# First attention: the division by the sums moved from VectorE to a ScalarE copy of the used columns and a GpSimd power and product

## Chip, cores and metric

One core of one Trainium2 chip. The metric is the device time of one launch in microseconds; the time is the median of the runs. One more execution, recorded by the profiler, gives the profile and the trace; its own time stands beside them below.

## The reference

Four layers follow each other, each added to its normalised input. Only the first attention is touched, and the time of the others counts with it:

```python
def _L0_attn_ref(x, ln_gamma, ln_beta, w_qkv, b_qkv, w_out, b_out):    # x: 4 x 1024 x 128, 16 heads of 8
    residual = x
    h = (x - mean(x)) * rsqrt(var(x) + 1e-05) * ln_gamma + ln_beta
    q, k, v = split_heads(h @ w_qkv + b_qkv)
    scores = einsum('bhqd,bhkd->bhqk', q, k) / sqrt(8)
    attn = softmax(scores)
    out = einsum('bhqk,bhkd->bhqd', attn, v)
    return residual + merge_heads(out) @ w_out + b_out

x = L0_attn_x
x = x + _L0_attn_ref(_layernorm(x), ...)
x = x + _L0_ffn_ref(_layernorm(x), ...)     # a shared expert and 8 routed ones, the best 2 of each row
x = x + _L1_attn_ref(_layernorm(x), ...)    # differential attention, 8 heads
x = x + _L1_ffn_ref(_layernorm(x), ...)     # linear layers on values quantised to 4 bits
```

The softmax is exp(score - maximum) divided by the sum of the exponentials. The kernel multiplies the undivided exponentials with the values and divides the result: each head has 8 columns of results and one column of sums.

## The kernel before

**Engines and order.** All four compute engines and the DMA queue of SyncE run through one list of steps (`plan_all`). Each engine takes from it, in this order, the steps in which it has a part, and every step's part stands in a function of the step's name, one per engine. Engines meet through semaphores: `SIGNALS` says which step raises which and by how much, `READ` says which signal tells that a step's PSUM bank has been read, so that the bank's next user may write it. All waits are counts worked out from the list. An engine never runs past a wait.

**The planner.** In the first attention time is counted in slots. A slot has one `maxima` step and, six steps of eight slots later, one `scores` step. `hook(s, slot, step)` puts a step at a given slot. Steps named in `BEHIND_SUMS`, `divide` among them, are held back and put directly behind the next `burst`, at most two at a time. `FOLLOWS` names steps that the planner adds a number of slots after another one has been put (`later`, `tick`). PSUM banks are given out in a ring: `maxima` and the other steps in `RINGED` share four banks (0 to 3), `scores` and the steps in `RINGED_ACT` share three (5 to 7), and bank 4 collects the results.

**Units.** A unit `u` (0 to 15) is one block of 1024 rows (`b = u // 4`) and four of its sixteen heads (`gr = u % 4`). It has these steps:

- `maxima(u, t, j, half)`, 64 in all: TensorE multiplies 128 queries of head j with 512 keys (L1705), VectorE takes the maximum of each row from PSUM (L1274, tile a_mx). `row1(u, c)` joins them (L1281), `row2(u, c)` turns them on TensorE (L1711) and ScalarE copies them out twice (L828, L829); `row2_low` subtracts the rounded copy on GpSimd (L2071) and writes both into the queries' extra rows by two DMAs (L2188). The scores of the next unit wait for these.
- `scores(u, hs, j)`, 64: TensorE (L1717), then ScalarE's exponential from PSUM into tile a_PT (L836). In the last half unit two of them are joined into a `pair` of 1024 columns (L1727, L844).
- `burst(u, c, k)`: TensorE multiplies the exponentials of mostly three tiles with values and a column of ones (L1743). After the last burst of each half c, ScalarE copies the collected results to tile a_OT (L851).
- `divide(u, r)`, two for each unit and so 32: TensorE turns 512 columns of a_OT by four transposes into a ring bank (L1751): 4 row tiles of 4 heads of 32 columns, of which 8 are results, the ninth is the sum, and the others aren't used. VectorE takes the reciprocals of the 16 sums (L1288, tile a_rc) and multiplies the 128 results with them into tile a_Oa (L1292).
- For the last unit of a block, `turn_o(b, r)`: TensorE turns a_Oa (L1758), ScalarE copies (L857), and `out_project(b, r)` multiplies (L1766) and adds to the residual on VectorE (L1300).

**What lies beside it.** The next block's norms are worked out during its predecessor's second unit: statistics on VectorE (`ln_stats` L1222, `ln_gather` L1232, L1239), a power of 8 columns on GpSimd (L2041), and `ln_apply` on GpSimd (L1117), four steps of two instructions each. GpSimd also has `residual` (L2054, L2057), `turn_h` (L2065) and the splitting of the expert weights (L2084, L2086).

**The end of the stage.** Steps left over when the slots end are put among the first steps of the experts: `divide(15, 1)` behind item 1, `turn_o(3, 1)` behind item 3 and the first `down`, and `out_project(3, 1)` behind item 5. An expert `item` is six products (L1810), a silu on ScalarE (L885), for routed experts a product on GpSimd (L2095), a product on VectorE (L1366); `halves` splits the result on ScalarE (L891) and VectorE (L1373), and `down` multiplies it (L1821).

Of the kernel before, what the change touches and what calls it, by code (L numbers as in the profile page):

```python
# [7 lines left out]
ALU = mybir.AluOpType  # L8
# [109 lines left out]
class Tally:  # L118
# [45 lines left out]
    "row2": lambda u, c: [(2, ("row2_low", u, c))],  # L164
    "ln_apply": lambda who, b, k: [(8, ("residual", b))] if (who, k) == ("x", 3) else [],
# [9 lines left out]
def snapped(on_dve):  # L175
# [26 lines left out]
    "divide": {"a_ot_pe": 1, "a_rc": 1, "a_on": 1},  # L202
# [76 lines left out]
    "divide": lambda *a: [("a_on", "divide", *a)],  # L279
# [304 lines left out]
def memory(nc, io):  # L584
# [74 lines left out]
    m.rc = [sb(f"a_rc{i}", [128, 4, 4]) for i in range(2)]  # L659
    m.nb = sb("a_nb", [128, NT])  # L660
# [106 lines left out]
def a_free(v, *step):  # L767

    return [v.at("a_oe", *half_sums(NU - 1, 0)), v.at("a_oe", *half_sums(NU - 1, 1)), v.at("a_st", "pair", NU - 1, 15, 1),
            v.now("a_add", *step), v.now("a_rc", *step)]  # L770


def scalar_engine(e, w, v, m):
# [72 lines left out]
    def burst(u, c, k):  # L846
        if ("burst", u, c, k) == half_sums(u, c):
            w.wait_ge(*at("a_pv", "burst", u, c, k))
            if u:
                w.wait_ge(*at("a_ot_pe", "divide", u - 1, c))  # L850
            e.activation(m.OT[:, 512 * c:512 * c + 512], P[:, 4, :], ACT.Copy).then_inc(m.S["a_oe"])  # L851

# [213 lines left out]
    parts = dict(first=first, first_hn=first_hn, turn_h=turn_h, project=project, row2=row2, scores=scores, pair=pair, burst=burst,  # L1066
# [90 lines left out]
def vector_engine(e, w, v, m):  # L1157
# [3 lines left out]
    def bank(*step):  # L1161
        return P[:, v.plan.bank[step], :]
# [120 lines left out]

    def divide(u, r):
        b, gr = divmod(u, 4)
        vw = bank("divide", u, r).rearrange("p (t j d) -> p t j d", t=4, j=4)
        w.wait_ge(*at("a_ot_pe", "divide", u, r))
        e.reciprocal(m.rc[r][:, :, :], vw[:, :, :, 8]).then_inc(m.S["a_rc"])  # L1288
        w.wait_ge(*at("a_rc", "divide", u, r))
        if b:  # L1290
            w.wait_ge(*at("a_oc_pe", "turn_o", b - 1, r))
        e.tensor_tensor(m.Oa[:, 4 * r:4 * r + 4, 32 * gr:32 * gr + 32].rearrange("p t (j d) -> p t j d", j=4),  # L1292
                        vw[:, :, :, 0:8], m.rc[r][:, :, :].unsqueeze(3).to_broadcast([128, 4, 4, 8]),
                        ALU.mult).then_inc(m.S["a_on"])
# [346 lines left out]
    def l_down(i):  # L1641
# [6 lines left out]
                 divide=divide, out_project=out_project, m_turn_x=m_turn_x,  # L1648
# [13 lines left out]
def tensor_engine(e, w, v, m):  # L1662
# [91 lines left out]
    def turn_o(b, r):  # L1754
        ps = bank("turn_o", b, r)
        w.wait_ge(*at("a_on", "divide", 4 * b + 3, r))
        for i in range(4):
            tt = e.transpose(ps[:, 128 * i:128 * i + 128], m.Oa[:, 4 * r + i, :], ident)  # L1758
        tt.then_inc(m.S["a_oc_pe"])
# [251 lines left out]
def gpsimd_engine(e, w, v, m):  # L2011
# [7 lines left out]
    def first():  # L2019
        e.memset(m.zero[:, :], 0.0).then_inc(m.S["a_fill"])  # L2020
        for h, done in ((0, 9), (1, 18), (0, 30), (1, 45)):
            c = slice(4 * h, 4 * h + 4)
            if done == 45:
                w.wait_ge("a_two", 1)
                w.wait_ge("a_fill", 1)
                e.tensor_scalar(m.one[:, :], m.zero[:, :], m.two[:, 0:1], 0.0, ALU.add, ALU.add).then_inc(m.S["a_fill"])
            w.wait_ge("a_first_dve", done)
            w.wait_ge("mh", 1)
            e.tensor_tensor(m.rs[:, c], m.ve[:, c], m.mh[:, c], ALU.pow).then_inc(m.S["a_first_pool"])

# [29 lines left out]
    def turn_h(b, c):  # L2060
        cs = slice(512 * c, 512 * c + 512)
        if b:
# [3 lines left out]
                            ALU.subtract).then_inc(m.S["a_hh"])  # L2066

# [63 lines left out]
    def l_norm():  # L2131
        for i in range(2):
# [5 lines left out]
                 turn_h=turn_h, row2_low=row2_low, small_weights=small_weights, split=split, item=item,  # L2138
# [219 lines left out]
```

## Time and profile before

| what | value |
|---|---|
| time, median of 3 runs | 2808.52 us (2808.43 to 2811.03) |
| profiled execution: its time | 2812.24 us |
| profiled execution: span of the instructions | 2810.5 us |
| TensorE (PE) busy | 2698.6 us, 96% |
| VectorE (DVE) busy | 2414.7 us, 86% |
| ScalarE (ACT) busy | 2031.1 us, 72% |
| GpSimd (POOL) busy | 1484.0 us, 53% |
| first attention | about 0 to 770 us |

The profile names engines PE (matmul), PEld (weight load), DVE, ACT, POOL and SPq (issues of SyncE's DMA queue). A busy share is the time in which an engine runs an instruction; matmuls overlap, so a busy PE need not be at its peak, and VectorE's and ScalarE's instructions overlap a little too: the next may start before the recorded end of the one before. Idle time ahead of an instruction is put down to what released it.

### The profile page before, as it was taken

To read this page: it belongs to the slowest core of one execution; us is meant where nothing else is said; L and a number is where in the kernel's file an instruction comes from. 1 tells how busy PE (TensorE), PEld (TensorE's weight loads), DVE (VectorE), ACT (ScalarE), POOL (GpSimd) and SP (SyncE) were. 2 spreads that over 40 slices of the span, in tenths; PEclk is the share of its full clock that TensorE was granted. 3 is DMA by queue.
4 is the path that set the end of the run, shared out by engine and by line. 5 is a ranking of instruction groups with operands and counts; after the bars stand their busy time and mean duration, and the time that the engine had idled before them with its cause. 6 is when DMAs were issued, how large, how long until landed. Compare 5 with 4: busy or idle time off the path is not lost.

```text
span 2810.5 us, 45813 instructions
## 1 busy us (share of the span) xinstructions
PE 2698.6 (96%) x16263; PEld 1980.0 (70%) x16263; DVE 2414.7 (86%) x4394; ACT 2031.1 (72%) x4477; POOL 1484.0 (53%) x1076
## 2 busy tenths in 40 slices
PE   6999999999999999999999999999999999999996
PEld 3333333333377777888888888888898888898895
DVE  7999999999688887788888978988888988888986
ACT  2888888888855556777777777777777777777773
POOL 2311203100055555567677667676767776766763
PEclk9999999999999999999999999999999999999997
DMA  4121021200112220000000000000000000000000
GB/s 132 37 67 37 28 82 37 73 32 17 50 38 82 89 61 9 1 1 1 1 1 3 3 1 3 3 1 3 3 1 3 3 1 3 3 3 1 3 3 6
DMA packets 41316, 65.18 MB, mean 23 GB/s; under 512 B 5176, under 2 KB 15992, under 8 KB 41088
## 3 DMA queue, kind: packets, MB, share of 16 engines
q1 hardware_dynamic: 41088, 62.26, 6.9%
q8 instruction: 129, 2.11, 0.3%
q14 instruction: 99, 0.81, 0.1%
HBM read 45.86 MB, written 15.86 MB: 22 GB/s over the span
## 4 chain that ended last, share of the span: by engine, by line
PE 63%; DVE 26%; issue 5%; ACT 3%; POOL 2%; DMA 0%; SPq 0%; DVEq 0%; ACTq 0%; POOLq 0%
PE P L1881 16%; PE P L1743 10%; PE P L1906 9%; PE P L1705 7%; DVE c_nm L1440 6%; PE P L1892 5%; PE P L1810 4%; DVE c_DT L1465 4%; DVE a_mx L1274 3%; PE P L1915 3%; PE P L1821 2%; PE P L1717 2%; PE P L1864 2%; DVE c_Tl L1473 1%; DVE d_tc L1548 1%
## 5 line engine op out<-in xcount | busy, mean ns | idle before, releaser
L1440 DVE TENSOR_REDUCE c_nm<-P 128x1 f32<-128x1024 f32 x512 | 622.2, 1215 | 106.8 <-PE P L1881 105.0
L966 ACT ACTIVATE c_P<-P,c_nm 128x1024 f32<-128x1024 f32 x512 | 572.4, 1118 | 181.1 <-DVE c_nm L1440 180.4
L1274 DVE TENSOR_REDUCE a_mx<-P 128x1 f32<-128x512 f32 x1024 | 628.1, 683 | 17.1 <-PE P L1705 15.4
L2104 POOL TENSOR_TENSOR c_P<-c_P,c_P 128x1024 f32<-128x1024 f32 (+1 forms) x256 | 617.5, 2412 | 21.3
L836 ACT ACTIVATE a_PT<-P 128x512 f32<-128x512 f32 x976 | 515.3, 598 | 109.6 <-PE P L1717 99.7
L2102 POOL TENSOR_SCALAR c_P<-c_P,c_rr 128x1024 f32<-128x1024 f32 (+1 forms) x256 | 296.8, 1160 | 443.3 <-DVE c_rr L1452 443.2
L1906 PE MATMUL P<-c_DT,c_xkh 128*128 128x256 f32 x2048 | 390.4, 284 | 2.7 <-DVE c_DT L1465 2.7
L1881 PE MATMUL P<-c_xth,c_Th 128*128 128x512 f32 x1024 | 365.4, 438 | 18.1 <-ACT c_P L966 18.1
L1743 PE MATMUL P<-a_PT,a_Vp 128*32 128x512 f32 x2048 | 367.3, 605 | 1.2 <-DVE a_Vp L1261 0.5
L1465 DVE TENSOR_TENSOR c_DT<-P,c_DT 128x512 fp32r<-128x512 f32 x512 | 348.5, 681 | 9.3 <-ACT c_DT L977 8.8
L1906 PEld LDWEIGHTS P<-c_DT,c_xkh 128*128 128x128 f32 x2048 | 327.6, 191 | 5.7 <-DVE c_DT L1465 5.7
L1892 PE MATMUL P<-ident,c_P 128*128 128x128 f32 x2048 | 308.9, 273 | 21.0 <-DVE c_DT L1465 16.8
L1881 PE MATMUL P<-c_xtl,c_Th 128*128 128x512 f32 x1024 | 320.9, 394 | 0.0
L1881 PE MATMUL P<-c_xth,c_Tl 128*128 128x512 f32 x1024 | 319.7, 393 | 0.0
L1705 PEld LDWEIGHTS P<-a_Ks,a_Qs 32*128 32x128 f32 x1024 | 125.3, 187 | 273.6 <-DVE a_mx L1274 220.7
L1705 PE MATMUL P<-a_Ks,a_Qs 32*128 32x512 f32 x1024 | 294.4, 492 | 9.8 <-DMA a_Qs<-qk_scratch 4.8
L977 ACT ACTIVATE c_DT<-P 128x512 fp32r<-128x512 f32 x512 | 303.5, 593 | 0.0
L1717 PE MATMUL P<-a_Qs,a_Ks 32*128 32x512 f32 x976 | 293.9, 486 | 7.3 <-ACT a_hT L813 3.9
L1906 PE MATMUL P<-c_DT,c_xkl 128*128 128x256 f32 x1024 | 289.6, 283 | 0.0
L1892 PEld LDWEIGHTS P<-ident,c_P 128*128 128x128 f32 x2048 | 241.7, 140 | 52.0 <-DVE c_DT L1465 24.9
L2071 POOL TENSOR_TENSOR a_mT<-a_mT 16x128 fp32r<-16x128 f32 x32 | 14.4, 450 | 489.8 <-ACT a_mT L829 489.8
L2095 POOL TENSOR_TENSOR b_sg<-b_sg,b_cwB 128x512 f32<-128x512 f32 x128 | 177.0, 1386 | 171.0 <-ACT b_sg L885 171.0
(245 smaller groups left out, 5149.8 us busy)
## 6 DMA issues: line engine op xcount, KB each, us to landing
b_cwB<-cw_scratch SPq DMA_DIRECT2D x64, 256.0 KB, 5.0
qk_scratch<-a_nh SPq DMA_DIRECT2D x32, 256.0 KB, 3.3
a_Ks<-qk_scratch SPq DMA_DIRECT2D x32, 256.0 KB, 3.0
a_Qs<-qk_scratch SPq DMA_DIRECT2D x32, 256.0 KB, 3.9
c_stg<-in_cw SPq DMA_DIRECT2D x8, 640.0 KB, 4.7
qk_scratch<-a_nl SPq DMA_DIRECT2D x16, 256.0 KB, 3.5
b_stg<-in_moe SPq DMA_DIRECT2D x9, 384.0 KB, 3.1
out<-xres SPq DMA_DIRECT2D x15, 128.0 KB, 1.8
```

What stands on the lines that cost most here:

```text
L836: e.activation(m.PT[:, j, hs % 4, :], bank("scores", u, hs, j), ACT.Exp, scale=SCALE).then_inc(m.S["a_exp"])
L966: e.activation(m.P1[s][n % 4][:, :], P[:, k:k + 2, :].rearrange("p c k -> p (c k)"), ACT.Exp, bias=m.nm[:, n % 4, s:s + 1], accum_out=m.sm ...
L1274: e.tensor_reduce(m.mx2[u % 2][:, t // 4, j, t % 4, half:half + 1], bank("maxima", u, t, j, half), AX, ALU.max).then_inc(m.S["a_max_dve"])
L1440: e.tensor_reduce(m.nm[:, n % 4, s:s + 1], P[:, k:k + 2, :].rearrange("p c k -> p (c k)"), AX, ALU.max, negate=True).then_inc(m.S["c_nm"])
L1465: e.tensor_tensor(lo, bank("turn", n, half).rearrange("p (t q) -> p t q", t=4), hi.bitcast(F32), ALU.subtract).then_inc(m.S["c_dl"])
L1705: e.matmul(ps, m.Qs[u % 3][r, 128 * t:128 * t + 128], m.Ks[u % 3][r, 512 * half:512 * half + 512], start=True, stop=True).then_inc(m.S["a_ ...
L1717: e.matmul(ps, m.Ks[u % 3][r, 128 * kt:128 * kt + 128], m.Qs[u % 3][r, 512 * c:512 * c + 512], start=True, stop=True).then_inc(m.S["a_st"])
L1743: tt = e.matmul(O[32 * j:32 * j + 32, :], m.Vp[b % 2][:, at_v:at_v + 32], m.PT[:, j, hs % 4, :], start=(kt == 0), stop=(kt == 7))
L1881: tt = e.matmul(ps[:, c, :], a[:, s, qs], x[:, 512 * c:512 * c + 512], start=(i == 0), stop=(i == 2))
L1892: tt = e.transpose(ps[:, 128 * i:128 * i + 128], m.P1[0][n % 4][:, 128 * kt:128 * kt + 128], ident)
L1906: tt = e.matmul(ps[:, 0:256], x[:, 128 * kt:128 * kt + 128], m.DT[p % 2][l][:, kt, :], start=(kt == 0 and j == 0), stop=(kt, j) == (7, 2))
L2104: e.tensor_tensor(p0, p0, p1, ALU.add).then_inc(m.S["c_D"])
```

## The change

`divide` keeps its transposes on TensorE, and its part on VectorE is gone. A new step `divide_out` follows two slots later. On ScalarE it copies the nine used columns of each head (128 x 144 values) from the PSUM bank to a new tile a_heads, which frees the bank. On GpSimd it raises the 16 sums to the power -1 (the exponent comes from a new tile a_minus, filled once) and multiplies the 128 results with them into a_Oa. `turn_o` and what frees the memory of this stage wait for GpSimd's product instead of VectorE's. The planner's list is otherwise as it was.

```diff
--- before.py
+++ after.py
@@ -162,6 +162,7 @@
 
 FOLLOWS = {
     "row2": lambda u, c: [(2, ("row2_low", u, c))],
+    "divide": lambda u, r: [(2, ("divide_out", u, r))],
     "ln_apply": lambda who, b, k: [(8, ("residual", b))] if (who, k) == ("x", 3) else [],
     "choose": lambda b: [(1 + k // 3, ("choose_step", b, k)) for k in range(15)],
     "c_turn_x": lambda b, c: [(1, ("c_turn_low", b, c))],
@@ -199,7 +200,8 @@
     "scores": {"a_st": 1, "a_exp": 1},
     "pair": {"a_st": 1, "a_exp": 1},
     "burst": lambda u, c, k: {"a_pv": 1, "a_oe": 1} if k == len(BURSTS[u, c]) - 1 else {"a_pv": 1},
-    "divide": {"a_ot_pe": 1, "a_rc": 1, "a_on": 1},
+    "divide": {"a_ot_pe": 1},
+    "divide_out": {"a_heads": 1, "a_rc": 1, "a_on": 1},
     "turn_o": {"a_oc_pe": 1, "a_oc_act": 1},
     "out_project": {"a_op_pe": 1, "a_add": 1},
     "small_load": {"b_w": 48},
@@ -276,7 +278,7 @@
     "scores": lambda *a: [("a_exp", "scores", *a)],
     "pair": lambda *a: [("a_exp", "pair", *a)],
     "burst": lambda u, c, k: [("a_oe", *half_sums(u, 1))],
-    "divide": lambda *a: [("a_on", "divide", *a)],
+    "divide": lambda *a: [("a_heads", "divide_out", *a)],
     "turn_o": lambda *a: [("a_oc_act", "turn_o", *a)],
     "out_project": lambda *a: [("a_add", "out_project", *a)],
     "m_turn_x": lambda *a: [("b_xl", "m_turn_x", *a)],
@@ -657,6 +659,8 @@
     m.nm0 = [[sb(f"a_nm{i}_{c}", [128, 16]) for c in range(2)] for i in range(2)]
     m.mT = [[sb(f"a_mT{i}_{c}", [16, 2, 128], F32R) for c in range(2)] for i in range(2)]
     m.rc = [sb(f"a_rc{i}", [128, 4, 4]) for i in range(2)]
+    m.heads = [sb(f"a_heads{i}", [128, 4, 4, 9]) for i in range(2)]
+    m.minus = sb("a_minus", [128, 4, 4])
     m.nb = sb("a_nb", [128, NT])
     assert top <= SB_END, top
 
@@ -767,7 +771,7 @@
 def a_free(v, *step):
 
     return [v.at("a_oe", *half_sums(NU - 1, 0)), v.at("a_oe", *half_sums(NU - 1, 1)), v.at("a_st", "pair", NU - 1, 15, 1),
-            v.now("a_add", *step), v.now("a_rc", *step)]
+            v.now("a_add", *step), v.now("a_on", *step)]
 
 
 def scalar_engine(e, w, v, m):
@@ -850,6 +854,13 @@
                 w.wait_ge(*at("a_ot_pe", "divide", u - 1, c))
             e.activation(m.OT[:, 512 * c:512 * c + 512], P[:, 4, :], ACT.Copy).then_inc(m.S["a_oe"])
 
+    def divide_out(u, r):
+        w.wait_ge(*at("a_ot_pe", "divide", u, r))
+        if u:
+            w.wait_ge(*at("a_on", "divide_out", u - 1, r))
+        e.activation(m.heads[r][:, :, :, :], bank("divide", u, r).rearrange("p (t j d) -> p t j d", t=4, j=4)[:, :, :, 0:9],
+                     ACT.Copy).then_inc(m.S["a_heads"])
+
     def turn_o(b, r):
         w.wait_ge(*at("a_oc_pe", "turn_o", b, r))
         if b:
@@ -1280,18 +1291,6 @@
             w.wait_ge(*at("a_mt_pe", "row2", u - 2, c))
         e.tensor_reduce(m.nm0[u % 2][c][:, :], m.mx2[u % 2][:, c].rearrange("p j t h -> p (j t) h"), AX, ALU.max,
                         negate=True).then_inc(m.S["a_nm"])
-
-    def divide(u, r):
-        b, gr = divmod(u, 4)
-        vw = bank("divide", u, r).rearrange("p (t j d) -> p t j d", t=4, j=4)
-        w.wait_ge(*at("a_ot_pe", "divide", u, r))
-        e.reciprocal(m.rc[r][:, :, :], vw[:, :, :, 8]).then_inc(m.S["a_rc"])
-        w.wait_ge(*at("a_rc", "divide", u, r))
-        if b:
-            w.wait_ge(*at("a_oc_pe", "turn_o", b - 1, r))
-        e.tensor_tensor(m.Oa[:, 4 * r:4 * r + 4, 32 * gr:32 * gr + 32].rearrange("p t (j d) -> p t j d", j=4),
-                        vw[:, :, :, 0:8], m.rc[r][:, :, :].unsqueeze(3).to_broadcast([128, 4, 4, 8]),
-                        ALU.mult).then_inc(m.S["a_on"])
 
     def out_project(b, r):
         xs = m.xres[:, 8 * b + 4 * r:8 * b + 4 * r + 4, :].rearrange("p t c -> p (t c)")
@@ -1753,7 +1752,7 @@
 
     def turn_o(b, r):
         ps = bank("turn_o", b, r)
-        w.wait_ge(*at("a_on", "divide", 4 * b + 3, r))
+        w.wait_ge(*at("a_on", "divide_out", 4 * b + 3, r))
         for i in range(4):
             tt = e.transpose(ps[:, 128 * i:128 * i + 128], m.Oa[:, 4 * r + i, :], ident)
         tt.then_inc(m.S["a_oc_pe"])
@@ -2027,6 +2026,7 @@
             w.wait_ge("a_first_dve", done)
             w.wait_ge("mh", 1)
             e.tensor_tensor(m.rs[:, c], m.ve[:, c], m.mh[:, c], ALU.pow).then_inc(m.S["a_first_pool"])
+        e.memset(m.minus[:, :, :], -1.0).then_inc(m.S["a_fill"])
 
     def ln_gather(who, b, k):
         if k == 0:
@@ -2065,6 +2065,18 @@
             e.tensor_tensor(m.hTl[:, cs], m.hT[:, cs], m.hTh[:, cs].bitcast(F32),
                             ALU.subtract).then_inc(m.S["a_hh"])
 
+    def divide_out(u, r):
+        b, gr = divmod(u, 4)
+        w.wait_ge(*at("a_heads", "divide_out", u, r))
+        w.wait_ge("a_fill", 3)
+        e.tensor_tensor(m.rc[r][:, :, :], m.heads[r][:, :, :, 8], m.minus[:, :, :], ALU.pow).then_inc(m.S["a_rc"])
+        w.wait_ge(*at("a_rc", "divide_out", u, r))
+        if b:
+            w.wait_ge(*at("a_oc_pe", "turn_o", b - 1, r))
+        e.tensor_tensor(m.Oa[:, 4 * r:4 * r + 4, 32 * gr:32 * gr + 32].rearrange("p t (j d) -> p t j d", j=4),
+                        m.heads[r][:, :, :, 0:8], m.rc[r][:, :, :].unsqueeze(3).to_broadcast([128, 4, 4, 8]),
+                        ALU.mult).then_inc(m.S["a_on"])
+
     def row2_low(u, c):
         t = m.mT[u % 2][c]
         w.wait_ge(*at("a_mt_act", "row2", u, c))
```

## Rows read from the trace of the kernel before

**Rows 1.** The page: shares of the chain that ended last, by engine.

```profile
PE 63%; DVE 26%; issue 5%; ACT 3%; POOL 2%; DMA 0%; SPq 0%; DVEq 0%; ACTq 0%; POOLq 0%
```

**Rows 2.** Groups by line, VectorE, 0 to 900 us: count, busy us, mean ns, idle before.

```profile
L1274 DVE TENSOR_REDUCE a_mx<-P 128x1 f32<-128x512 f32 x1024 | 628.1, 683 | 17.1 <-PE P L1705 15.4 <-DVE a_nm L1281 0.2
```

**Rows 3.** Timeline round divide (13, 0): start us, length us, engine, line, [idle before].

```profile
669.76 0.66 PE L1751 MATMUL P<-ident,a_OT 128*128 128x128 f32 x4
...
670.46 0.26 DVE L1288 RECIPROCAL a_rc<-P 128x16 f32<-128x16 f32 x1
...
671.41 1.08 ACT L836 ACTIVATE a_PT<-P 128x512 f32<-128x512 f32 x2
...
672.00 0.49 PE L1705 MATMUL P<-a_Ks,a_Qs 32*128 32x512 f32 x1
...
672.55 0.50 PE L1717 MATMUL P<-a_Qs,a_Ks 32*128 32x512 f32 x1
```

**Rows 4.** Timeline round divide (4, 1), with norm statistics in VectorE's queue.

```profile
292.11 0.66 PE L1751 MATMUL P<-ident,a_OT 128*128 128x128 f32 x4
...
293.33 0.26 DVE L1288 RECIPROCAL a_rc<-P 128x16 f32<-128x16 f32 x1
...
293.83 0.68 DVE L1274 TENSOR_REDUCE a_mx<-P 128x1 f32<-128x512 f32 x1
```

**Rows 5.** Groups by line and form, GpSimd, whole span: two powers, one product.

```profile
L2041 POOL TENSOR_TENSOR ln_rs<-ln_ve,ln_mh 128x8 f32<-128x8 f32 x14 | 23.2, 1656 | 71.3 <-DVE ln_ve L1239 71.3
...
L2129 POOL TENSOR_TENSOR d_vr<-d_vr,ln_mh 128x2 f32<-128x2 f32 x15 | 10.7, 714 | 19.6 <-DVE d_vr L1572 19.6
...
L1154 POOL TENSOR_TENSOR d_tn<-d_tn,d_tc 128x128 f32<-128x128 f32 x2 | 0.9, 455 | 2.4 <-DVE d_tc L1550 2.4
```

**Rows 6.** Timeline, ScalarE: the two copies of the row of maxima.

```profile
278.03 0.27 ACT L828 ACTIVATE a_mT<-P 16x128 fp32r<-16x128 f32 x1
...
278.20 0.25 ACT L829 ACTIVATE a_mT<-P 16x128 f32<-16x128 f32 x1
```

**Rows 7.** Timeline from 271 us; its DMA bytes, 278 to 283 us, 40 slices.

```profile
271.41 4.69 POOL L1117 TENSOR_SCALAR xn<-xres,ln_mv,ln_rs 128x128 f32<-128x128 f32 x6
...
278.53 0.45 POOL L2071 TENSOR_TENSOR a_mT<-a_mT 16x128 fp32r<-16x128 f32 x1 [2.43 <-ACT a_mT L829]
...
GB/s 0 0 0 0 0 0 0 0 0 0 0 0 0 0 0 0 0 37 29 0 0 0 62 4 0 123 147 123 197 270 344 344 270 344 393 320 197 49 25 0
...
282.11 0.49 PE L1717 MATMUL P<-a_Qs,a_Ks 32*128 32x512 f32 x1
```

**Rows 8.** Timeline, 755 to 773 us: the last two turns of the result.

```profile
755.80 4.96 ACT L844 ACTIVATE a_PT<-P 128x1024 f32<-128x1024 f32 x5
...
760.24 0.66 PE L1758 MATMUL P<-ident,a_Oa 128*128 128x128 f32 x4
...
770.87 1.29 POOL L2095 TENSOR_TENSOR b_sg<-b_sg,b_cwB 128x512 f32<-128x512 f32 x1 [29.34 <-ACT b_sg L885]
...
771.52 0.63 ACT L891 ACTIVATE b_hh<-b_hf 128x512 fp32r<-128x512 f32 x1 [0.73 <-DVE b_hf L1366]
...
772.75 0.60 PE L1758 MATMUL P<-ident,a_Oa 128*128 128x128 f32 x4
```

**Rows 9.** Timeline, one gap of TensorE; busy times and granted clock (first bare number).

```profile
810.84 0.41 PE L1791 MATMUL P<-ident,b_lgT 8*128 8x8 f32 x4 [1.49 <-DVE b_lgT L1317]
...
812.00:816.00 4.00, 4.00 (x12) 2.53 (x11) 1.81 (x5) 3.25 (x6) 1.28 (x1) 0.57 0.00 0
```

**Rows 10.** Timeline, GpSimd and VectorE side by side at two places.

```profile
814.36 1.28 POOL L2095 TENSOR_TENSOR b_sg<-b_sg,b_cwB 128x512 f32<-128x512 f32 x1 [8.27 <-ACT b_sg L885]
...
814.83 1.35 DVE L1373 TENSOR_TENSOR b_hl<-b_hf,b_hh 128x512 fp32r<-128x512 f32 x1 [2.03 <-ACT b_hh L891]
...
784.93 1.64 POOL L2041 TENSOR_TENSOR ln_rs<-ln_ve,ln_mh 128x8 f32<-128x8 f32 x1 [1.72 <-DVE ln_ve L1239]
...
785.05 0.69 DVE L1373 TENSOR_TENSOR b_hl<-b_hf,b_hh 128x512 fp32r<-128x512 f32 x1 [0.20 <-ACT b_hh L891]
```

More of the change, by code:

```diff
@@ L1064, in l_gate @@
         tanh(bank("l_gate", i), i)
-    parts = dict(first=first, first_hn=first_hn, turn_h=turn_h, project=project, row2=row2, scores=scores, pair=pair, burst=burst,
+    parts = dict(first=first, first_hn=first_hn, turn_h=turn_h, project=project, row2=row2, scores=scores, pair=pair, burst=burst, divide_out=divide_out,
                  turn_o=turn_o, m_turn_x=m_turn_x, choose=choose, spread=spread, item=item, halves=halves, down=down,
@@ L1647, in vector_engine @@
                  turn_h=turn_h, values=values, project=project, maxima=maxima, row1=row1,
-                 divide=divide, out_project=out_project, m_turn_x=m_turn_x,
+                 out_project=out_project, m_turn_x=m_turn_x,
                  route=route, route_turn=route_turn, choose_step=choose_step, product=product, halves=halves, finish=finish, small=small,
@@ L2137, in gpsimd_engine @@
     parts = dict(one=one, first=first, ln_gather=ln_gather, ln_apply=ln_apply, residual=residual,
-                 turn_h=turn_h, row2_low=row2_low, small_weights=small_weights, split=split, item=item,
+                 turn_h=turn_h, divide_out=divide_out, row2_low=row2_low, small_weights=small_weights, split=split, item=item,
                  combine=combine,
```

## The prediction

> **What bounds the kernel now.** I read the page first: of the chain that ended last TensorE has 63%, VectorE 26%, ScalarE 3% [rows 1]. That chain covers four stages. The change touches only the first attention (up to about 770 us of 2810.5) and the first microseconds of the stage behind it, so I went to the groups by line for that stretch: VectorE's 1024 row maxima (L1274) take 628.1 us there [rows 2]. VectorE looks full, and a change that takes its divides away looks like a gain of 32 times half a microsecond. Whether it is one is read in the timeline round each divide, instruction by instruction: who waits for whom at that place.
>
> The rhythm there: TensorE issues three pairs (a maxima product, a scores product), then a burst, and so on. The maxima go round four PSUM banks that VectorE frees, the scores round three banks that ScalarE's exponentials free. The divide's four transposes stand behind a burst and take one of the four banks.
>
> Round divide (13, 0) the transposes end at 669.76 + 0.66 = 670.42, and the reciprocal starts at 670.46, 0.04 us later: VectorE had run dry and was waiting for TensorE [rows 3]. On the other side two exponentials run back to back from 671.41 to 672.49, and the last scores product of the group that starts at 672.00 goes at 672.55, at once when the second of them has freed its bank [rows 3]. So at this place ScalarE's exponentials, not VectorE, hold TensorE. I found this pattern at 14 of the 32 divides. At three of them (one in each block that has the next norm's statistics in VectorE's queue) it is the reverse: transposes end at 292.77, the reciprocal starts only at 293.33, the next maximum at 293.83, and VectorE is never dry up to the next divide [rows 4].
>
> **What the change does, part by part.**
>
> *VectorE loses reciprocal and product.* The pair holds it 0.50 us (293.33 to 293.83 [rows 4]). Where VectorE was dry, the next maximum needs a product that TensorE starts only at the end of the transposes and that lasts 0.50 us, so it could start 0.07 us earlier at most, and the bank that TensorE asks for next is ScalarE's: I book nothing. At the three full places the 0.50 us is real and is kept, since TensorE waits for VectorE's banks behind it: 3 x 0.5 = -1.5 us. At the other divides VectorE runs dry again within one half unit: nothing.
>
> *ScalarE gains a copy of 144 columns per divide.* By the planner's rule (two slots behind the divide) it stands in its queue behind one exponential and ahead of the next two, which are those that TensorE waits for. The trace has no 144-column copy; the nearest are the two 128-column copies of the row of maxima, 0.27 and 0.25 us long, with starts 0.17 us apart (278.03, 278.20) [rows 6]. 16 more columns add little: 0.19 us of queue, bounded by 0.17 and, if nothing overlaps, 0.28. At the 14 places both exponentials, both scores and the burst behind them come 0.19 us later. Nothing gives it back: up to the next divide, TensorE's and ScalarE's waits there lead from one to the other, and VectorE runs dry as well. 14 x 0.19 = +2.7 us (2.4 to 3.9). At three divides there is half that slack left: 3 x 0.1 = +0.3. Two more stand in the stretch of paired exponentials at the end, where ScalarE is the engine that runs back to back: 2 x 0.19 = +0.4. At six, beside turns and projections, the scores start later than the exponentials allow: 0. The bank of the divide is now freed by the copy, at 671.41 + 0.27 = 671.68; the product that takes it next starts at 672.00 [rows 3]: hidden, by 0.3 us.
>
> *GpSimd gains a power and a product.* A power costs it 714 ns for 2 columns and 1656 ns for 8, so 157 ns a column; 16 columns: 1656 + 8 x 157 = 2.9 us. The product of 128 columns: 455 ns [rows 5]. Together 3.4 us. Bounds: 1.7 + 0.46 (all beyond 8 columns free) and 3.3 + 0.9 (two powers of 8, a product in runs of 8 columns at double price). GpSimd has idle time for it in most units; what counts is who is queued behind. First its own row subtraction (L2071), whose DMAs the next scores wait for. In three units (4b, the first half) it is queued behind the norm's applications: three of the four run ahead of it, 1.56 us each, from 271.41 to 276.10, then GpSimd waits for ScalarE until 278.53 [rows 7]. The divide goes between the first application and the others, so all behind it moves: first application to 273.0, copy ready at 273.6 (an estimate: 1.3 us behind the transposes, as in rows 3), power and product to 277.0, two applications to 280.2. The subtraction starts 1.6 us late. Its bytes were over at about 281.0 (DMA view, slices of 0.125 us) and the score that needs them started at 282.11 [rows 7]: 1.1 us are hidden, 0.5 us are not. 3 x 0.5 = +1.5 us (0 to 4). In all other units 3.4 us fit ahead of the subtraction.
>
> *TensorE's turn of the result (turn_o) now waits for GpSimd.* For seven of eight there is cover. The tightest is (3, 0) among the paired exponentials: its copy stands ahead of the one at 755.80, so power and product are through at 755.80 + 0.27 + 3.4 = 759.5, and the transposes start at 760.24 [rows 8]. If the cover goes, every microsecond is one of TensorE's. The eighth, (3, 1), has none. It stands in the expert stage, and its divide goes: ScalarE's conversion at 771.52, 0.63 long, behind that the copy (to 772.4), GpSimd is free by then (its item ends at 772.16), power to 775.3, product to 775.8. Before, the transposes started at 772.75, at once behind TensorE's own work [rows 8]. TensorE is in order and full there, so it stands for 3.1 us (1.9 to 3.9), and what waits for it (all items) moves by that.
>
> *The clock.* One place of the trace compares: TensorE idle 1.49 us ahead of 810.84, and the granted clock in 812 to 816 us is 0.57 on average, 1.2 GHz for most of it [rows 9]. A gap of twice that length should do the same once more. That average makes it 3.4 us at the lower level, in which half of the work is lost: 1.6 us (0 if it doesn't fall).
>
> One rule speaks against the change at the same place. At 814.36 GpSimd starts a product of two SBUF tensors for 1.28 us, and VectorE's subtraction of two SBUF tensors, started at 814.83, takes 1.35 us instead of about 0.69; but beside GpSimd's power of 784.93 one takes 0.69, as alone [rows 10]. The Trainium skill (SBUF — State Buffer, Who interferes with whom) says that the two engines share one port pair and that whoever comes first holds it for the whole instruction. By that, VectorE's subtraction would hold the last divide's power back by up to 0.5 us, and the sum would be 8.6 instead of 8.1. The first pair of rows agrees with it, the second doesn't, and I leave it out. The maxima read PSUM and have no part in it.
>
> **The sum.** -1.5 + 2.7 + 0.3 + 0.4 + 1.5 + 3.1 + 1.6 = +8.1 us. Against the profiled execution (2812.24 us: span 2810.5 and 1.7 around it) that is 2820.3; the median of the runs, 2808.52, lies 3.7 us lower, so 2816.6 us.
>
> **Rivals.**
> 1. *VectorE was the bound after all, and the change is faster.* Place: every divide. For it: 628 us of maxima in some 700 us [rows 2]. Against it: the reciprocal waits for the transposes [rows 3]. If TensorE could come earlier by as much as VectorE is relieved, 32 x 0.5 = -16, plus 3.1 and 1.6 at the end: 2797. It decides on the fast side if more than some 20 divides pay. Chance 0.08.
> 2. *ScalarE's copy finds room, the rest stands.* For it: ScalarE has idle time in each group. Against it: not where the copy is put. Then -1.5 + 1.5 + 3.1, with the clock's 1.6 or without: 2811.6 to 2813.2, within the noise. Chance 0.27.
> 3. *GpSimd's power is much slower with this exponent (5 us).* Nothing in the trace shows the exponent -1. Then 2.1 us more in three units, at the last divide, and 1.5 at the one before it: 8.1 + 9.9, 2826.5. Chance 0.07.
> My forecast has the remaining 0.58; its own range, from the bounds of the terms, is 2811.5 to 2821.
>
> **How the numbers follow.** The forecast and rival 3 are slower, save the forecast's lower end; rival 2 is the same; rival 1 faster. A measurement of this kernel tells 0.2%, 5.6 us, from no change, so the same is 2802.9 to 2814.1. Slower: 0.07 + about nine tenths of 0.58, less what I may have missed: 0.59. Same: 0.27 and a tenth of the forecast: 0.32. Faster: 0.09. The range leaves out rivals 1 and 3 and reaches down over rival 2 with a little room for gains that I booked at nothing: 2808 to 2821.
>
> **What would show it.** In the profile after: (a) VectorE's maxima as long as before, but with more idle time ahead of them, released by TensorE; (b) the divides of a quiet unit 0.19 us further apart, scores products released by the exponentials; (c) power 2.9 us, product 0.46 us, the copy 0.27 us; (d) row subtractions of units 1, 5 and 9 some 1.6 us later against the divide; (e) TensorE idle about 3 us ahead of the last turn of the result, near 776 us, and a fall of its clock behind that. The prediction is wrong if quiet divides come closer together than before, if no gap stands at (e), or if the power isn't near 2.9 us.

## The result, and the profile after

The changed kernel takes 2819.3 us (median of 7 runs, 2816.1 to 2821.43); the kernel before, run beside it, 2811.03 us (7 runs, 2808.43 to 2814.71). The ratio of the runs is 1.0026, with a 95% interval of 1.0016 to 1.0037: slower, by some 7 us. The profiled spans are 2810.5 before and 2817.2 after. The forecast of 2816.6 us was counted from 2808.52; the median of the kernel before, run beside the changed one, lies 2.5 us higher. Measured against forecast, the time is 2.7 us higher and the difference of the medians 8.3 us for 8.1.

The page of the changed kernel: busy time, and the shares of the chain that ended last (before, its shares were those of [rows 1]).

```profile
PE 2700.5 (96%) x16263; PEld 1984.6 (70%) x16263; DVE 2402.8 (85%) x4330; ACT 2034.1 (72%) x4509; POOL 1588.5 (56%) x1141
...
PE 62%; DVE 25%; issue 6%; ACT 3%; POOL 3%; DMA 1%; SPq 0%; DVEq 0%; ACTq 0%; POOLq 0%
```

The page's groups of the changed kernel, whole span: VectorE's row maxima, and GpSimd's new power. The maxima last as long as in [rows 2], 683 ns each; the idle time ahead of them has doubled, 33.7 us for 17.1, and TensorE ends 31.7 of it. VectorE was relieved and now waits more.

```profile
L1285 DVE TENSOR_REDUCE a_mx<-P 128x1 f32<-128x512 f32 x1024 | 629.3, 683 | 33.7 <-PE P L1704 31.7
...
L2072 POOL TENSOR_TENSOR a_rc<-a_heads,a_minus 128x16 f32<-128x16 f32 x32 | 93.6, 2924 | 320.3 <-ACT a_heads L861 320.3
```

Groups by line, GpSimd, 0 to 800 us of the changed kernel: the new product (count; busy us, mean ns; idle).

```profile
L2076 POOL TENSOR_TENSOR a_Oa<-a_heads,a_rc 128x128 f32<-128x128 f32 x32 | 13.0, 407 | 2.5
```

**A quiet divide.** Timeline of the changed kernel round divide (13, 0), the counterpart of [rows 3]. The copy stands where the prediction put it, and the exponentials behind it start 0.17 us after it. The scores product that waits for them starts 674.34 - 671.37 = 2.97 us behind the transposes; before it was 672.55 - 669.76 = 2.79. VectorE's first maximum now waits 0.41 us for TensorE instead of standing behind a divide.

```profile
671.37 0.66 PE L1750 MATMUL P<-ident,a_OT 128*128 128x128 f32 x4
...
672.50 0.69 DVE L1285 TENSOR_REDUCE a_mx<-P 128x1 f32<-128x512 f32 x1 [0.41 <-PE P L1704]
...
673.02 0.28 ACT L861 ACTIVATE a_heads<-P 128x144 f32<-128x144 f32 x1
673.19 2.56 ACT L840 ACTIVATE a_PT<-P 128x512 f32<-128x512 f32 x5
...
674.34 0.49 PE L1716 MATMUL P<-a_Qs,a_Ks 32*128 32x512 f32 x1
```

**A late row subtraction.** Timeline of the changed kernel, GpSimd and TensorE from 271 us, the counterpart of [rows 7]. The power waits 0.68 us for the copy, then power, product and two applications stand ahead of the row subtraction. It starts at 280.59, and the score that needs its DMA starts at 283.45, while TensorE had nothing left to do. The last line gives the DMA bytes of this kernel, 279 to 285 us, in 40 slices of 0.15 us: the subtraction's own are the two pairs ahead of a larger transfer (where no such transfer runs, in the kernel before at 676 to 681 us, two such pairs stand alone), and the last of them are over at 283.05, 0.40 us ahead of the score.

```profile
271.83 1.58 POOL L1128 TENSOR_SCALAR xn<-xres,ln_mv,ln_rs 128x128 f32<-128x128 f32 x2
274.09 2.93 POOL L2072 TENSOR_TENSOR a_rc<-a_heads,a_minus 128x16 f32<-128x16 f32 x1 [0.68 <-ACT a_heads L861]
277.10 0.41 POOL L2076 TENSOR_TENSOR a_Oa<-a_heads,a_rc 128x128 f32<-128x128 f32 x1
277.49 3.12 POOL L1128 TENSOR_SCALAR xn<-xres,ln_mv,ln_rs 128x128 f32<-128x128 f32 x4
280.59 0.45 POOL L2083 TENSOR_TENSOR a_mT<-a_mT 16x128 fp32r<-16x128 f32 x1
...
283.45 0.46 PE L1716 MATMUL P<-a_Qs,a_Ks 32*128 32x512 f32 x1 [0.71 <-DMA a_Qs<-a_mT]
...
GB/s 0 0 0 0 0 0 0 0 0 0 0 0 0 0 0 0 0 0 0 0 0 31 24 0 0 41 14 0 102 184 102 143 225 307 451 410 328 246 103 21
```

**The last divide.** Timeline of the changed kernel, 770 to 779 us, the counterpart of [rows 8], then a later gap as in [rows 9]. TensorE stands still for 3.35 us and is released by GpSimd's product.

```profile
773.47 0.63 ACT L902 ACTIVATE b_hh<-b_hf 128x512 fp32r<-128x512 f32 x1 [0.73 <-DVE b_hf L1365]
...
774.00 0.27 ACT L861 ACTIVATE a_heads<-P 128x144 f32<-128x144 f32 x1
774.13 0.69 DVE L1372 TENSOR_TENSOR b_hl<-b_hf,b_hh 128x512 fp32r<-128x512 f32 x1 [0.70 <-ACT b_hh L902]
...
774.36 3.23 POOL L2072 TENSOR_TENSOR a_rc<-a_heads,a_minus 128x16 f32<-128x16 f32 x1 [0.25 <-ACT a_heads L861]
...
777.66 0.41 POOL L2076 TENSOR_TENSOR a_Oa<-a_heads,a_rc 128x128 f32<-128x128 f32 x1
...
778.21 1.09 PE L1757 MATMUL P<-ident,a_Oa 128*128 128x128 f32 x4 [3.35 <-POOL a_Oa L2076]
...
817.88 0.41 PE L1790 MATMUL P<-ident,b_lgT 8*128 8x8 f32 x4 [1.49 <-DVE b_lgT L1316]
```

Busy times by stretch, changed kernel (us, PE, PEld, DVE, ACT, POOL, granted clock, DMA share, GB/s): behind the gap the clock is 0.57 on average over 4 us, 1.2 GHz for most of them.

```profile
778.00:782.00 4.00, 3.79 (x12) 3.22 (x13) 1.32 (x4) 1.71 (x3) 2.00 (x3) 0.57 0.04 15
```

### The profile page after: what moved, and what is told of

Read it like the earlier page. It is cut to its first block, busy times and chain, and to the rows that moved or that the text cites. A ratio compares the mean times of both kernels' runs of the same rounds, so it can differ in the third digit from the quotient of the medians.

```text
span 2817.2 us, 45855 instructions
## 1 busy us (share of the span) xinstructions
PE 2700.5 (96%) x16263; PEld 1984.6 (70%) x16263; DVE 2402.8 (85%) x4330; ACT 2034.1 (72%) x4509; POOL 1588.5 (56%) x1141
## 4 chain that ended last, share of the span: by engine, by line
PE 62%; DVE 25%; issue 6%; ACT 3%; POOL 3%; DMA 1%; SPq 0%; DVEq 0%; ACTq 0%; POOLq 0%
PE P L1880 16%; PE P L1742 9%; PE P L1905 9%; DVE c_nm L1439 6%; PE P L1704 6%; PE P L1891 5%; PE P L1809 4%; DVE c_DT L1464 4%; PE P L1914 3%; DVE a_mx L1285 3%; PE P L1820 2%; PE P L1716 2%; PE P L1863 2%; DVE c_Tl L1472 1%; DVE d_tc L1547 1%
## 5 line engine op out<-in xcount | busy, mean ns | idle before, releaser
L1285 DVE TENSOR_REDUCE a_mx<-P 128x1 f32<-128x512 f32 x1024 | 629.3, 683 | 33.7 <-PE P L1704 31.7
L2072 POOL TENSOR_TENSOR a_rc<-a_heads,a_minus 128x16 f32<-128x16 f32 x32 | 93.6, 2924 | 320.3 <-ACT a_heads L861 320.3
```

The lines of the kernel that those rows point to most:

```text
L1285: e.tensor_reduce(m.mx2[u % 2][:, t // 4, j, t % 4, half:half + 1], bank("maxima", u, t, j, half), AX, ALU.max).then_inc(m.S["a_max_dve"])
```

## The ruler

Whole times of single executions of one kernel differ by some 6 us (before: 2808.43 to 2814.71), and the profiles differ outside the places that the change touches: the first divide's transposes start anywhere from 92.1 to 94.8 us in the ten profiles of this study, and from 1200 us on short low-clock stretches are there in some and not in others. So I measure one stretch: from the first divide's transposes to the router's transposes at 810.84 [rows 9], which every kernel has at the same place of its list (817.88 after). Within it I group the 31 intervals between the starts of consecutive divides' transposes in the timeline: A, behind (0, 0), (4, 0), (8, 0); B, behind (0, 1), (4, 1), (8, 1); C, behind (7, 1); Q, twelve quiet ones (behind (2, 1), (3, 0), (6, 1), (7, 0), (10, 1), (11, 0), (11, 1), (12, 0), (12, 1), (13, 0), (13, 1), (14, 0)); O, the other twelve. Then T, from the last divide to the last turn of the result, and K, from there to the router's transposes. All in us, as differences to the kernel before, whose stretch is 810.84 - 92.44 = 718.40 (T 3.88, K 38.09):

| kernel | A | B | C | Q | O | T | K | all | ratio of the whole times, 95% |
|---|---|---|---|---|---|---|---|---|---|
| changed | +2.53 | -1.48 | -0.39 | +1.26 | +0.04 | +3.52 | +1.58 | +7.06 | 1.0026 (1.0016 to 1.0037) |
| no divide | -0.28 | -1.47 | -0.37 | -0.57 | -0.23 | 0.00 | -0.02 | -2.94 | 0.9987 (0.9979 to 0.9996) |
| copy only | -0.07 | -1.46 | -0.39 | +1.40 | +0.21 | 0.00 | -0.01 | -0.32 | 0.9995 (0.9986 to 1.0004) |
| two copies | +0.42 | -1.49 | -0.40 | +3.42 | +1.29 | +0.01 | -0.03 | +3.22 | 1.0010 (1.0000 to 1.0019) |
| short power | -0.10 | -1.47 | -0.39 | +1.30 | -0.01 | +0.83 | 0.00 | +0.16 | 1.0001 (0.9992 to 1.0010) |
| last back | +2.50 | -1.46 | -0.39 | +1.24 | -0.04 | +0.01 | -0.03 | +1.83 | 1.0011 (1.0002 to 1.0020) |
| three back | -0.02 | -1.50 | -0.38 | +1.23 | -0.03 | +3.51 | +1.44 | +4.25 | 1.0025 (1.0016 to 1.0034) |
| four back | -0.04 | -1.47 | -0.38 | +1.29 | -0.01 | 0.00 | -0.04 | -0.65 | 0.9999 (0.9990 to 1.0008) |
| four moved | +0.03 | -1.15 | -0.39 | +0.05 | -0.01 | 0.00 | -0.02 | -1.49 | 0.9995 (0.9986 to 1.0004) |

The changed kernel's terms add to 7.06 with rounding, its span grew by 6.7. Columns that no edit touches repeat within 0.1 us (K within 0.14: 1.58 and 1.44), so differences of single intervals can be read. In every row but one the ruler's sum lies within the interval of the whole times; the exception is three back, of which more below.

## The experiments

**1. No divide** (relief_alone), **and the copy only** (relief_copy). The first is the kernel before without VectorE's two operations; the second adds the ScalarE copy to it. The edits, the first against before (the memset is GpSimd's, once), the second against the changed kernel (the function is GpSimd's power and product):

```diff
-        e.reciprocal(m.rc[r][:, :, :], vw[:, :, :, 8]).then_inc(m.S["a_rc"])
-        ...
-                        ALU.mult).then_inc(m.S["a_on"])
+        e.memset(m.Oa[:, :, :], 1.0).then_inc(m.S["a_fill"])
```

```diff
-    def divide_out(u, r):
-    ...
-        w.wait_ge(*at("a_on", "divide_out", 4 * b + 3, r))
+        w.wait_ge("a_fill", 3)
```

> The kernel before, with VectorE's reciprocal and product left out at all 32 divides and nothing in their place: no copy, no power, no product (the result's tile is filled once with ones, so the division by the sums and what it feeds are left out). Theory (VectorE is on the path only behind the second divide of units 0, 4 and 8): those three intervals between divides come 0.5 us shorter, the quiet ones stay within 0.05 us of before, together -1.5 us against the kernel before. Rival A (the relief is worth 0.09 us at each quiet divide too, and in the changed kernel it paid for half of the copy): quiet intervals 0.09 shorter, together -1.5 - 14 x 0.09 = -2.8 us. Rival B (VectorE is the bound at every divide and the copy hid that): 0.5 us shorter at each, -16 us, 2795 us.

> The changed kernel with the ScalarE copy of the used columns but without GpSimd's power and product (tile of the result filled once with ones; the division is left out). What it stands above the kernel without any divide is the price of the copy alone. Theory (copy costs its 0.19 us of queue at each of 14 quiet divides, and something gives 0.09 back only where VectorE is relieved, so that the kernel without a divide is itself 0.09 faster per place): +2.7 to +3.0 us above it. Rival (the copy costs only 0.10 us per quiet divide): +1.3 to +1.7 us above it. Against the kernel before: near 0 (-0.5 to +0.5) by either. Against the changed kernel: -7.2 us (2.5 of the late row subtractions, 3.5 of the last turn, 1.25 of the clock), no gap near 776 us and no clock fall behind it. If more than 1 us of these 7.2 stays, ScalarE's copy and not GpSimd was its cause.

Measured: no divide, -2.94 us on the ruler. B is -1.47, as the theory has it; C is -0.37, where it had nothing; each quiet interval is 0.05 shorter (Q -0.57 over twelve), each of A 0.09 (-0.28), and O together 0.23. So neither the theory (-1.5) nor rival B (-16): in total rival A (-2.8), though with 0.05 rather than 0.09 per quiet place and the rest at (7, 1), in A and in O. VectorE is not the bound, but it isn't free of charge between its full places either.

The copy costs 2.62 us (-0.32 against -2.94): near the theory's 2.7 to 3.0, not the rival's 1.3 to 1.7. In Q it is 1.97 over 12 = 0.16 per place; the other 0.65 are in A (0.21) and O (0.44). The timeline shows the same shift; kernel without a divide first (scores product 670.48 - 667.70 = 2.78 us behind the transposes):

```profile
667.70 0.66 PE L1739 MATMUL P<-ident,a_OT 128*128 128x128 f32 x4
...
670.48 0.50 PE L1705 MATMUL P<-a_Qs,a_Ks 32*128 32x512 f32 x1
```

Timeline with the copy only (672.65 - 669.68 = 2.97):

```profile
669.68 0.66 PE L1748 MATMUL P<-ident,a_OT 128*128 128x128 f32 x4
...
671.33 0.29 ACT L859 ACTIVATE a_heads<-P 128x144 f32<-128x144 f32 x1
671.50 2.57 ACT L840 ACTIVATE a_PT<-P 128x512 f32<-128x512 f32 x5
...
672.65 0.50 PE L1714 MATMUL P<-a_Qs,a_Ks 32*128 32x512 f32 x1
```

Against the changed kernel the copy-only kernel is 7.38 us shorter: 2.60 in A, 3.52 in T, 1.59 in K, and 0.3 the other way in B to O (Q -0.14, O -0.17), which no experiment here explains. What GpSimd costs is all in three intervals and at the end.

**2. Two copies** (copy_twice). The copy-only kernel with each copy made twice.

```diff
+        e.activation(m.heads[2 + r][:, :, :, :], bank("divide", u, r).rearrange("p (t j d) -> p t j d", t=4, j=4)[:, :, :, 0:9],
+                     ACT.Copy)
```

> The kernel with the copy and nothing on GpSimd, but with every copy made twice (second destination unused). Theory (ScalarE's exponentials are what TensorE waits for at the 14 quiet divides, and a 144-column copy takes 0.17 to 0.19 us of the queue behind another ScalarE operation): each quiet interval 0.17 to 0.2 us longer than with one copy, 14 x 0.18 = +2.5 us, and the three half-quiet ones +0.1 to 0.2 each, together +2.7 to +3.2 us. Rival A (the first copy cost only what was left after a slack, the second costs its full 0.28): 14 x 0.28, +3.9 us or more. Rival B (the copy cost its 0.16 not by ScalarE's queue but by the later release of the divide's bank): the second copy costs as much again only if that bank is waited for; then maxima products, not scores products, stand waiting behind the divide.

Measured: Q grows by 2.02, 0.17 per place, as the theory has it and not 0.28. The total grows by 3.54, above the theory's 2.7 to 3.2, since ten more intervals (A three times, seven in O) grow by 0.11 to 0.19, where the first copy had cost A and O 0.65 in all: the slack that had hidden part of the first copy there is used up. Timeline of this kernel: both copies and the exponentials start 0.17 us apart, and the scores product comes 675.21 - 672.07 = 3.14 us behind the transposes. 2.78, 2.97, 3.14: each copy moves it by its pitch in ScalarE's queue. The burst ahead of them ends at 673.32 + 1.06 = 674.38, and the group's first products are recorded from 674.31, with no wait for the divide's bank between, so rival B falls.

```profile
672.07 0.66 PE L1750 MATMUL P<-ident,a_OT 128*128 128x128 f32 x4
...
673.32 1.06 PE L1742 MATMUL P<-a_PT,a_Vp 128*32 128x512 f32 x6
...
673.71 0.29 ACT L859 ACTIVATE a_heads<-P 128x144 f32<-128x144 f32 x1
673.88 0.30 ACT L861 ACTIVATE a_heads<-P 128x144 f32<-128x144 f32 x1
674.05 2.58 ACT L840 ACTIVATE a_PT<-P 128x512 f32<-128x512 f32 x5
...
674.31 0.49 PE L1704 MATMUL P<-a_Ks,a_Qs 32*128 32x512 f32 x1
...
675.21 0.50 PE L1716 MATMUL P<-a_Qs,a_Ks 32*128 32x512 f32 x1
```

**3. The last divide back** (back_last), **three back** (back_three), **four back** (back_four). The changed kernel with the divides named in BACK left on VectorE. The edit (the new function is VectorE's, with its two operations as before), with BACK = {(15, 1)}, {(0, 0), (4, 0), (8, 0)}, or all four:

```diff
-    "divide": lambda u, r: [(2, ("divide_out", u, r))],
+    "divide": lambda u, r: [] if (u, r) in BACK else [(2, ("divide_out", u, r))],
...
+    def divide(u, r):
+        if (u, r) not in BACK:
+            return
```

> The changed kernel with the last divide (15, 1) alone back on VectorE. Theory (TensorE's last turn of the result waits for GpSimd's 3.6 us, and the clock falls because of that gap): the gap of 3.35 us and the low clock near 778 us are both gone, -3.5 - 1.25 = -4.8 us against the changed kernel, 2814.5 us. Rival A (something else of the expert stage would hold TensorE there by then, such as ScalarE's conversion or the load of the items): the gap shrinks to 1.5 to 3 us and only 0.5 to 2 us come back. Rival B (the clock would have fallen at this place or a little later anyway): -3.5 us and the low stretch is still there.

> The changed kernel with the divides (0, 0), (4, 0) and (8, 0) back on VectorE: those that put GpSimd's power and product ahead of the norm's applications. Theory (the row subtraction comes 2 us late behind them and the first scores product waits for its DMA): the intervals from these divides to the next come back from 0.84 us above the kernel before to within 0.1 of it; row subtraction as early against the divide as before; 3 x 0.82 = -2.5 us against the changed kernel. Rival (half of the 0.84 comes from ScalarE's copies or from the applications, which are late for others than the scores): the intervals stay 0.3 to 0.5 above before, -1.0 to -1.5 us. Second rival (VectorE is as full here as behind the second divide of the unit, and its 0.5 us comes back): intervals 0.5 above before, -1.0 us, and the maxima rather than the DMA release the scores.

> The changed kernel with (0, 0), (4, 0), (8, 0) and (15, 1) back on VectorE: both prices of GpSimd gone, all else as changed. Theory (the parts add): intervals as with three back, no gap and no clock fall at the last turn; from the first divide to the last turn of the result -0.7 us against the kernel before (-1.5 - 0.4 at the four paying places, about +1.2 for the copies at the quiet ones), and 6.2 us less than the changed kernel. Rival (with the three divides back, time comes back elsewhere, as the whole kernel with three back showed no gain): no difference to the changed kernel but the last turn's 5.1 us.

Measured: with the last one back, T returns from +3.52 to +0.01 and K from +1.58 to -0.03, -5.23 us in all (expected -4.8, of it 1.25 for the clock), and nothing else moves. Both rivals fall: no gap is left, and no low stretch. The busy times of this kernel by stretch: TensorE is full and the clock is 1.00 where it had been 0.57.

```profile
776.00:780.00 4.00, 4.00 (x20) 3.25 (x19) 3.40 (x8) 2.83 (x5) 2.48 (x3) 1.00 0.55 197
```

With three back, A returns from +2.53 to -0.02 (-2.81 on the whole ruler), by the theory and neither rival: the 0.5 us of VectorE's divide costs nothing there, and half of the price does not stay. Gap and clock fall are still there, with the same 3.35 us:

```profile
777.93 1.09 PE L1777 MATMUL P<-ident,a_Oa 128*128 128x128 f32 x4 [3.35 <-POOL a_Oa L2096]
```

With four back the parts add: -0.65 on the ruler (expected -0.7), 7.71 us below the changed kernel (my 6.2 was too little). One thing stays open: the whole time with three back (ratio 1.0025) doesn't show the 2.8 us that its trace shows on the ruler. Its span is 7.5 us longer than before, and only 4.25 of that are on the ruler. In its profile the opening ahead of the first divide, which the edit does not reach, was 2.4 us longer than before, and TensorE's clock came up at 71 instead of 65 us; another 0.9 us lie behind the ruler. Four back had nearly the same opening (+1.9) and a ratio of 0.9999. Of the eleven executions with three back, nine take 2818.07 to 2820.36 us; the other two, 2813.84 and 2814.29, lie 2.3 us and 2.2 us below the two fastest of the changed kernel (2816.1 and 2816.5), near what the ruler shows. Whether such openings belong to these kernels or to single executions, one profile each can't tell.

**4. A short power** (short_power). The changed kernel with the power replaced by a multiplication; all waits and handovers stay.

```diff
-        e.tensor_tensor(m.rc[r][:, :, :], m.heads[r][:, :, :, 8], m.minus[:, :, :], ALU.pow).then_inc(m.S["a_rc"])
+        e.tensor_tensor(m.rc[r][:, :, :], m.heads[r][:, :, :, 8], m.minus[:, :, :], ALU.mult).then_inc(m.S["a_rc"])
```

> The changed kernel with GpSimd's power replaced by a multiplication of the same operands (the results are scaled wrongly: the reciprocal is left out). All handovers stay (copy, wait, two operations on GpSimd, wait of TensorE); only the 2.9 us of the power go, to some 0.3 us. Theory (the power's length is what costs): the intervals behind (0, 0), (4, 0) and (8, 0) fall from 0.85 above the kernel before to 0.1 or less, the gap ahead of the last turn of the result from 3.35 us to 0.6 to 0.9, and the clock does not fall behind it: -2.5 - 2.7 - 1.6 = -6.8 us against the changed kernel. Rival (the handovers cost: semaphores, the copy's place behind ScalarE's conversion, GpSimd's start): the intervals stay 0.4 or more above before, and the gap stays 1.5 us or more.

Measured: A -0.10, T +0.83 instead of +3.52, K 0.00; -6.90 us against the changed kernel (theory -6.8). Of T, 2.69 us are the power's length; 0.83 are what stays without it: the copy, the two short operations and the handovers. The timeline of this kernel: the gap is 0.65 us.

```profile
771.54 0.69 DVE L1372 TENSOR_TENSOR b_hl<-b_hf,b_hh 128x512 fp32r<-128x512 f32 x1 [0.70 <-ACT b_hh L902]
...
771.76 0.55 POOL L2072 TENSOR_TENSOR a_rc<-a_heads,a_minus 128x16 f32<-128x16 f32 x1 [0.22 <-ACT a_heads L861]
...
772.95 0.63 PE L1757 MATMUL P<-ident,a_Oa 128*128 128x128 f32 x4 [0.65 <-POOL a_Oa L2076]
```

**5. Four moved** (only_four). The same edit as in 3, with BACK all divides but the four that paid:

```diff
+BACK = {(u, r) for u in range(16) for r in range(2)} - {(0, 1), (4, 1), (7, 1), (8, 1)}
```

> The kernel before with only the divides (0, 1), (4, 1), (7, 1) and (8, 1) moved to ScalarE and GpSimd, the other 28 left on VectorE: those behind which the changed kernel was faster. Theory (gain and price lie at different divides, so the gain can be had alone): intervals behind the four -0.5, -0.5, -0.4, -0.5, all others within 0.05 of before, no gap at the last turn: -1.9 us against the kernel before. Rival (the gains at (0, 1), (4, 1), (8, 1) need VectorE to be ahead from the divides in front of them, which are back here): less than -1.0 us in all.

Measured: -1.49 us on the ruler; the whole time is 0.9995 of before (0.9986 to 1.0004), so it can't be told from before. Three of the four intervals gave what was expected (-0.50, -0.39, -0.49). Behind (4, 1) it was -0.16 instead of -0.49, which the theory of independent places (-1.9 in all) doesn't explain; the rival (less than -1.0) has the right sign at this one place and is wrong at (0, 1) and (8, 1). The timeline of this kernel has VectorE idle for 0.24 us there, which it does not with three back:

```profile
293.22 0.19 DVE L1297 TENSOR_REDUCE a_nm<-a_mx 128x16 f32<-128x32 f32 x1
293.65 0.69 DVE L1290 TENSOR_REDUCE a_mx<-P 128x1 f32<-128x512 f32 x1 [0.24 <-DVE a_nm L1297]
```

The same sign stands in the kernel before behind (7, 1), the place of column C, and is gone there once the divide is moved. Timeline of before:

```profile
429.62 0.19 DVE L1281 TENSOR_REDUCE a_nm<-a_mx 128x16 f32<-128x32 f32 x1
430.05 0.69 DVE L1274 TENSOR_REDUCE a_mx<-P 128x1 f32<-128x512 f32 x1 [0.24 <-DVE a_nm L1281]
```

What in the order of the queues brings it to one place or the other, no run here shows.

## Why the prediction held, and which terms were off

The forecast was +8.1 us; the ruler shows +7.06, the span +6.7. The signs that it named were all found: more idle time ahead of the maxima, the late row subtractions, the power at 2.92 us, the gap and the fall of the clock behind it; only the quiet divides are 0.10 us further apart instead of 0.19. Each cost was found at its place and for the reason given, if not at its size. What was missed is gain: half of what relieving VectorE brings. The near hit of the total is in part luck, since the errors cancel: relief elsewhere -1.5, the copy -0.8, the row subtraction +1.1, the last turn +0.4, and 0.3 us less in Q and O than the copy-only kernel would have, which add to -1.1.

- *Relief at three full places, -1.5.* Measured -1.47 (B). Right, to the place.
- *Relief elsewhere, nothing.* Wrong: another -1.5 (no divide: -2.94 in all). A fourth place, (7, 1), gave 0.37; I had looked for places where VectorE is never dry up to the next divide, and missed one that is full for a short time, with statistics right behind its divide. The rest are some 0.05 us at each quiet place (0.57 in all), 0.28 in A and 0.23 in O. At the quiet places "nothing gives it back" was too strong. Round (13, 0) the copy delays scores and burst by 0.18 us; but the burst after those, in the kernel before, came 674.74 - 672.98 = 1.76 us behind, and with the copy and without VectorE's divide 674.73 - 673.07 = 1.66: 0.10 us come back one group later. I had followed the chain for one group and inferred the rest.
- *The copy, 2.7 + 0.3 + 0.4 = 3.4.* Measured 2.62. The pitch is 0.17 us (the row gives 673.02 to 673.19), 0.16 to 0.17 on the interval: the lower bound was the value, since the copies of [rows 6] were the right neighbours and 16 more columns add nothing that can be seen. It is paid in full at 12 places, not 14 (1.97); A and O hold the other 0.65, for which the prediction had 0.7 elsewhere. The Trainium skill (ScalarE: Activation LUTs, What ACT_TABLE_LOAD costs) gives 186 ns plus 0.833 ns per column for an activation with immediate scale and bias, and an overlap of 93 ns back to back. By that the pitch would be 0.21 us, an estimate from that page; the trace has 0.17, and the trace decides.
- *Net at a quiet divide, +0.19.* Therefore +0.10 (Q +1.26 over twelve).
- *The late row subtraction, 1.5.* Measured 2.60 (A, changed against copy only). Its delay against the divide was right: (280.59 - 278.53) - (272.07 - 271.62) = 1.61 us, 272.07 being the start of the changed kernel's transposes and 271.62 that of before. The step that failed is the hidden part: I took the 1.1 us between the last bytes of the DMA and the score [rows 7] as slack. From the subtraction to a score that waits for nothing else it takes 283.45 - 280.59 = 2.86 us; before, it took 282.11 - 278.53 = 3.58, so the slack was 0.72, and 1.61 - 0.72 = 0.89, against 0.87 measured per place. The difference of 1.1 and 0.72 is the 0.40 us that pass in the changed kernel between the last bytes and the score that waits for them. The Trainium skill (DMA: Bandwidth & Descriptors, Anatomy of one DMA — SWDGE (gpsimd) path) says of GpSimd's path that a DMA's semaphore rises only once its last byte is confirmed in the target memory; this DMA goes through SP's queue, where the 0.40 us would fit the same, but no run here shows their cause.
- *TensorE waits at the last turn, 3.1.* Measured 3.52. Copy, power and product came in the order and at the distance predicted. The missing 0.4 is mostly something that I had left out: VectorE's subtraction of two SBUF tensors started at 774.13, the power at 774.36, and it took 3.23 us instead of 2.90. With the multiplication in its place the same happens: 0.55 us at this place, 0.22 elsewhere, again 0.33 more. In both, the added time ends 0.13 to 0.14 us ahead of the recorded end of VectorE's 0.69 us, and two so different lengths with one surcharge speak for a held start, not a slower rate. No run moves the subtraction away, so that it is this one that holds GpSimd is argued, not shown. With the measured 0.33 the term would have been 3.4. The rule that the prediction weighed (SBUF — State Buffer, Who interferes with whom, of the Trainium skill) agrees with the trace here: 0.33 us, where the prediction took up to 0.5 from it.
- *The clock, 1.6.* Measured 1.58 (K), and 1.44 with three back. It goes with the gap: 3.35 us brought it in both, 0.65 us and none did not. No run has the gap without the fall, so K is put down to the clock by the low stretch alone. The prediction's own step was rounded kindly: half of its 3.4 us is 1.7, not 1.6.
- *Rivals.* VectorE as the bound (-16): fell with the kernel without a divide. The copy finds room: not at the quiet places, where it costs 0.16 of its 0.17 us; of the changed kernel's net 0.10 the rest is VectorE's relief. A much slower power: it was 2.92 us on average, as extrapolated from [rows 5].

## What to carry to other kernels

An engine that looks full is worth relieving only where it holds the others; here the move of 32 divides helped at four, cost a little at twelve and much at four others. Such places were found by intervals between repeated landmarks, with each half of a move tried alone: 0.05 us per place is visible there and drowned in the whole time. Before work goes to a slow engine, ask who waits for the last instance of it: the steady state hid 3.4 us of GpSimd at 28 of 32 divides, and the one at the seam, with no work left to hide it, cost 5.1 of the 7 us. When you call a DMA hidden, count from the instruction that starts it to a consumer that really waits, not to its last byte.

## What the runs showed of the hardware

- A ScalarE copy of 144 columns lasts 0.28 us in the record but costs its queue 0.17 us, the same as one of 128 columns in 16 partitions [rows 6].
- GpSimd's power costs by the column: 0.71, 1.66 and 2.92 us for 2, 8 and 16 columns; a multiplication of the same 16 columns takes 0.22 us. The exponent is -1 in the last and -0.5 in the first two, and all three lie on one line of 157 ns a column.
- The same idle time of TensorE, 1.5 us ahead of the router's transposes, was followed by a low clock in six of the ten profiles and not in the other four; why, no run here shows. With it the next such transposes come 6.95 to 6.98 us later (before, 810.84 to 817.79), without it 6.61 or 6.62 (copy only, 811.18 to 817.79). So a fall of about the same length cost 0.35 us here and 1.58 us behind the last turn. The timelines show the difference: in the four profiles without it TensorE is idle again for 1.07 to 1.09 us ahead of those next transposes, waiting for VectorE, and in the six with it it isn't idle there. 1.07 + 0.35 is 1.42, near the 1.58: a fall cost what such idle time did not take up. Busy times, kernel with the copy only, the stretch of [rows 9], and from its timeline those next transposes:

```profile
812.00:816.00 4.00, 4.00 (x19) 2.81 (x18) 1.81 (x5) 3.96 (x7) 1.29 (x1) 1.00 0.00 0
...
817.79 0.41 PE L1788 MATMUL P<-ident,b_lgT 8*128 8x8 f32 x4 [1.07 <-DVE b_lgT L1314]
```
